# One load of second weights per step, another order of SyncE's transfers, and own buffers for the rows of half slots, in a kernel of attention and routed experts

## The reference

```python
# x: 4 x 1024 tokens of 256 features, float32
x = x + attn(layernorm(x))      # 16 heads of 16, rotary positions, causal, softmax, projection
x = x + experts(layernorm(x))

def experts(x):                 # 4096 tokens, 8 experts, 256 -> 1024 -> 256
    aff = x @ centroids.T
    assign = argmax(aff, axis=1)                 # one expert per token
    alpha = sigmoid(aff[assign])
    h = layernorm(x, ln_g[assign], ln_b[assign])
    y = x + relu(h @ w1[assign].T + b1[assign]) @ w2[assign].T + b2[assign]
    return alpha * y + (1 - alpha) * x
```

## Time and profile before

| | us |
|---|---|
| median of 3 runs (lowest, highest) | 881.75 (878.6, 885.98) |
| the profiled execution, its own time | 886.25 |
| its span, from the first to the last instruction | 884.5 |
| TensorE busy in the span | 812.1 (92%) |
| VectorE busy | 599.5 (68%) |
| ScalarE busy | 508.4 (57%) |
| GpSimd busy | 340.6 (39%) |
| mean granted clock of TensorE | 0.967 |

### The profile page before, as it was taken

How to read it: one execution, slowest core, us unless ns; L and a number is a source line. 1 busy time by engine, 2 the same in 40 slices (tenths; PEclk the granted TensorE clock), 3 DMA queues, 4 the chain that set the end, 5 groups by cost and what they waited for, 6 DMA issues and landing times. The chain is left out here.

```text
span 884.5 us, 24359 instructions
## 1 busy us (share of the span) xinstructions
PE 812.1 (92%) x8788; PEld 497.3 (56%) x8789; DVE 599.5 (68%) x1161; ACT 508.4 (57%) x1175; POOL 340.6 (39%) x476
## 2 busy tenths in 40 slices
PE   7999859889979999999999988777999999999984
PEld 4555423333334444443344335456999999999853
DVE  5888999779969999999999605754733333333342
ACT  4767427668858888888888892023333333333331
POOL 9999653233333433334343332524111111133211
PEclk9999979999989999999999999988899999999998
DMA  7578532543453343433335115865555555555550
GB/s 281 179 231 255 170 119 69 175 169 53 111 106 91 95 100 97 90 87 86 86 81 159 51 42 180 277 189 196 173 186 182 180 180 183 187 187 189 179 173 4
DMA packets 63355, 128.90 MB, mean 146 GB/s; under 512 B 16982, under 2 KB 44247, under 8 KB 56983
## 3 DMA queue, kind: packets, MB, share of 16 engines
q1 hardware_dynamic: 59094, 112.53, 42.9%
q0 software_dynamic: 4160, 15.03, 4.6%
HBM read 99.89 MB, written 22.98 MB: 139 GB/s over the span
## 5 line engine op out<-in xcount | busy, mean ns | idle before, releaser
L917 ACT ACTIVATE arena<-ps_pair 128x512 f32<-128x512 f32 (+2 forms) x640 | 317.9, 556 | 76.6 <-PE ps_pair L1240 73.7
L997 DVE TENSOR_REDUCE B_block_max<-ps_item 128x8 f32<-128x1024 f32 x288 | 335.4, 1217 | 37.4 <-PE ps_item L1144 37.1
L1240 PE MATMUL ps_pair<-q_stack,k_stack 99*32 99x512 bf16 (+7 forms) x3072 | 198.5, 334 | 9.4 <-DMA q_stack<-B_nm 6.7
L831 POOL TENSOR_SCALAR_AFFINE_SELECT arena<-arena 128x256 f32<-128x256 f32 x256 | 102.4, 409 | 160.2 <-ACT arena L917 158.5
L1257 PE MATMUL ps_pair<-arena,B_v_quad 128*32 128x512 f32 (+3 forms) x1536 | 157.0, 493 | 0.9 <-ACT B_oacc L936 0.7
L1240 PEld LDWEIGHTS ps_pair<-q_stack,k_stack 99*32 99x32 bf16 (+1 forms) x3072 | 69.1, 96 | 130.0 <-ACT arena L917 62.1
L2037 PEld LDWEIGHTS C_bank<-arena 128*128 128x128 f32 x1024 | 122.5, 196 | 5.2 <-ACT arena L1558 3.7
L2037 PE MATMUL C_bank<-arena 128*128 128x128 f32 x1024 | 123.0, 280 | 2.0 <-ACT arena L1558 2.0
L1144 PE MATMUL ps_item<-k_stack,q_stack 64*128 64x128 bf16 (+2 forms) x1280 | 108.2, 267 | 15.9 <-DVE B_block_max L997 8.9
L2061 PE MATMUL C_ps_p<-arena 128*128 x512 | 117.4, 381 | 3.2 <-issue 3.1
L1588 ACT ACTIVATE arena<-C_bank,ffn_columns 128x128 f32<-128x128 f32 x128 | 36.6, 368 | 116.8 <-PE C_bank L2037 108.0
(11 more groups left out here) (204 smaller groups left out, 777.0 us busy)
## 6 DMA issues: line engine op xcount, KB each, us to landing
arena<-in_w_exp SPq DMA_DIRECT2D x41, 1024.0 KB
qk_parts<-arena SPq DMA_DIRECT2D x32, 384.0 KB, 3.4
q_stack<-qk_parts SPq DMA_DIRECT2D x96, 128.0 KB, 3.3
k_stack<-qk_parts SPq DMA_DIRECT2D x64, 128.0 KB, 3.4
arena<-in_w_exp POOLq DMA_DIRECT2D x6, 1024.0 KB, 7.1
rows<-payload SPq DMA_DIRECT2D x32, 130.5 KB
arena<-in_x SPq DMA_DIRECT2D x8, 512.0 KB, 4.7
arena<-in_x_feat SPq DMA_DIRECT2D x8, 512.0 KB, 5.7
```

The costliest lines, as they stand in the source:

```text
L831: pool.affine_select(out=block_p, in_=block_p, compare_op=ALU.is_ge, fill=0.0, base=0, pattern=[[0, 2], [1, P]], channel_multiplier=-1).th ...
L917: act.activation(pr[s % PR][:, h:h + 2 * n - 1:2, 0:W], ps_s[(EXPS * Q.const + exps_to[s] + u) % R][:, 0:n * W].rearrange("p (h n) -> p h ...
L997: dve.tensor_reduce(bmx[:, g:QH:GH, first:first + 3 * gap + 1:gap], src[:, :, :].rearrange("p c (b n) -> p c b n", n=P), AX.X, ALU.max).th ...
L1240: mm = pe.matmul(bank[at:at + 32, :], ks[rows, r, half, bass.ds(g * SEQ + kb * P + at, 32)], qs[rows, r, half, bass.ds(g * SEQ + c * QW + ...
```

## The change

In attention, the six early loads of second weights go out one to a step (steps 1, 2, 3, 4, 5 and 14) instead of in pairs (1, 1, 2, 2, 14, 14), and in sub-step 4 instead of sub-step 2. SyncE's step issues the rows of maxima ahead of `place_out` instead of behind it, and `spread_inverse` ahead of the pad rows; these are written three in each of steps 5, 7 and 9 instead of nine in step 4. In the expert phase, each half slot has its own buffer for its rows and a semaphore of its own, and they are loaded one half slot a step in steps 24 to 30, behind the loads of the step, with no wait for a result.

```diff
+        half_rows = ctx.enter_context(nc.sbuf_tensor("half_rows", [P, HALVES, P + PAYW - DIM], F32))
+        def load_half_rows(sp, k):
+            at = sp.value_load(slot_tab[0:1, 1, bass.ds(FULL + k, 1)], min_val=0, max_val=DUMMY_ROW + HT)
+            sp.dma_start(half_rows[:, k, 0:P],
+                         pay_d[bass.ds(at, HT), 0:DIM].rearrange("t (a n) -> a t n", a=DC)).then_inc(s_rh[k], 16)
+            sp.dma_start(half_rows[:, k, P:P + PAYW - DIM],
+                         pay_d[bass.ds(at, HT), DIM:PAYW].unsqueeze(0).to_broadcast([DC, HT, PAYW - DIM])).then_inc(s_rh[k], 16)
...
-        early_at = (1, 1, 2, 2, 14, 14)
+        early_at = (1, 2, 3, 4, 5, 14)
+        W2_AT = 4
...
                     if n.const >= 3:
                         store_inverse(sp, n.const - 3)
-                    if n.const >= 2:
-                        place_out(sp, n.const - 2, out_ring(n.const - 2))
                     if n.within(NQ):

                         wait(sp, s_n3, n, 1, 1)
                         for half in range(2):
                             sp.dma_start(qs[SROWS[half]:SROWS[half] + MROWS, n.ring(R), half, :],
                                          nm[half * MAXR // 2:(half + 1) * MAXR // 2, :]).then_inc(s_row, 16)
+                    if n.const >= 2:
+                        place_out(sp, n.const - 2, out_ring(n.const - 2))
                     if n.const == 2:
                         load_bias_rows(sp)
-                    if n.const == 4:
-                        sp.wait_ge(s_pad0, 2)
-                        for e in range(NE + 1):
-                            sp.dma_start(pay_d[e * REGION:e * REGION + P, :], padrow).then_inc(s_pad, 16)
                     if n.const >= 3:
                         spread_inverse(sp, n.const - 3)
+                    if n.const in (5, 7, 9):
+                        if n.const == 5:
+                            sp.wait_ge(s_pad0, 2)
+                        for e in range(3 * (n.const - 5) // 2, 3 * (n.const - 5) // 2 + 3):
+                            sp.dma_start(pay_d[e * REGION:e * REGION + P, :], padrow).then_inc(s_pad, 16)
...
-                        if k == NM_AT + 1:
+                        if k == W2_AT:
...
-                    if S.within(NSLOT):
+                    if S.within(NSLOT) and not is_half(S):
...
+                    if n.reg is None and COPY_AT <= n.const < COPY_AT + HALVES:
+                        load_half_rows(sp, n.const - COPY_AT)
```

More of the change, by code:

```diff
@@ L347, in program @@
         rows = ctx.enter_context(nc.sbuf_tensor("rows", [P, RD, PAYW], F32))
+        half_rows = ctx.enter_context(nc.sbuf_tensor("half_rows", [P, HALVES, P + PAYW - DIM], F32))
+        s_rh = [sem(f"half_rows_loaded{k}") for k in range(HALVES)]
         def load_rows(sp, S):
-            at = sp.value_load(slot_tab[0:1, 1, bass.ds(S.value(), 1)], min_val=0,
-                               max_val=DUMMY_ROW + (HT if is_half(S) else 0))
-            if is_half(S):
-                sp.dma_start(rows[:, S.ring(RD), 0:HT * 2],
-                             pay_d[bass.ds(at, HT), 0:DIM].rearrange("t (a n) -> a t n", a=DC)).then_inc(s_rl[S.ring(RD)], 16)
-                sp.dma_start(rows[:, S.ring(RD), DIM:PAYW],
-                             pay_d[bass.ds(at, HT), DIM:PAYW].unsqueeze(0).to_broadcast([DC, HT, PAYW - DIM])).then_inc(s_rl[S.ring(RD)], 16)
-            else:
-                sp.dma_start(rows[:, S.ring(RD), :], pay_d[bass.ds(at, P), :]).then_inc(s_rl[S.ring(RD)], 16)
@@ new lines, in row_data, with row_scalar, wait_rows @@
+        def row_data(S):
+            return half_rows[:, S.const - FULL, 0:P] if is_half(S) else rows[:, S.ring(RD), 0:DIM]
+        def row_scalar(S, c):
+            if is_half(S):
+                return half_rows[:, S.const - FULL, c - P:c - P + 1]
+            return rows[:, S.ring(RD), c:c + 1]
+        def wait_rows(eng, S):
+            if is_half(S):
+                eng.wait_ge(s_rh[S.const - FULL], 32)
+            else:
+                wait_dma(eng, s_rl, S)
+        phase_route_experts(nc, x, pay_d, load_w1, load_rows, load_half_rows, row_data, row_scalar, wait_rows, w2s, w1b, s_w1, cols, b2, cst, ident, eps, slot_tab, col, b2r,
@@ L1273, in _, with phase_route_experts @@
                 steps(pe, emit)
-def phase_route_experts(nc, x, pay_d, load_w1, load_rows, rows, s_rl, w2s, w1b, s_w1, cols, b2, cst, ident, eps, slot_tab, col, b2r,
+def phase_route_experts(nc, x, pay_d, load_w1, load_rows, load_half_rows, row_data, row_scalar, wait_rows, w2s, w1b, s_w1, cols, b2, cst, ident, eps, slot_tab, col, b2r,
                         wp, bp3, ones3, xl, o_feat, room, spare_room, s_b3, out, gate,
@@ L1528, in normalize @@
                     if S.within(NSLOT):
-                        wait_rows(act, s_rl, S)
+                        wait_rows(act, S)
                         wait(act, s_tx, S, 1, -1)
                         wait(act, s_tl, S, 1, -1)
-                        row = rows[:, S.ring(RD), :]
                         n = P if is_half(S) else DIM
-                        act.activation(zz[:, S.ring(2), 0:n], row[:, 0:n], ACT.Identity, bias=row[:, COL_B:COL_B + 1],
-                                       scale=row[:, COL_S:COL_S + 1]).then_inc(s_zz, 1)
+                        act.activation(zz[:, S.ring(2), 0:n], row_data(S), ACT.Identity, bias=row_scalar(S, COL_B),
+                                       scale=row_scalar(S, COL_S)).then_inc(s_zz, 1)
                 for w in range(NP):
@@ L1604, in emit @@
                     if S.within(NSLOT):
-                        wait_rows(act, s_rl, S)
+                        wait_rows(act, S)
                         wait(act, s_res, S, 1, -1)
-                        act.activation(al[:, S.ring(2), 0:1], rows[:, S.ring(RD), COL_GATE:COL_GATE + 1], ACT.Exp,
+                        act.activation(al[:, S.ring(2), 0:1], row_scalar(S, COL_GATE), ACT.Exp,
                                        scale=-1.0).then_inc(s_ex, 1)
@@ L1833, in tail @@
                     if S.within(NSLOT):
-                        row = rows[:, S.ring(RD), :]
                         wait(dve, s_zz, S, 1, 1)
                         n = P if is_half(S) else DIM
-                        dve.scalar_tensor_tensor(out=row[:, 0:n], in0=zz[:, S.ring(2), 0:n], scalar=row[:, COL_K:COL_K + 1], in1=row[:, 0:n],
+                        dve.scalar_tensor_tensor(out=row_data(S), in0=zz[:, S.ring(2), 0:n], scalar=row_scalar(S, COL_K), in1=row_data(S),
                                                  op0=ALU.mult, op1=ALU.add).then_inc(s_tl, 1)
@@ L1870, in keep_ids @@
                 def keep_ids(S):
-                    at = rows[:, S.ring(RD), COL_ID:COL_ID + 1].bitcast(I32)
+                    at = row_scalar(S, COL_ID).bitcast(I32)
                     if is_half(S):
@@ L1924, in emit @@
                         dve.scalar_tensor_tensor(out=res[:, S.ring(2), 0:k], in0=y[:, S.ring(2), 0:k], scalar=al[:, S.ring(2), 2:3],
-                                                 in1=rows[:, S.ring(RD), 0:k],
+                                                 in1=row_data(S),
                                                  op0=ALU.mult, op1=ALU.add).then_inc(s_res, 1)
```

9 lines of the change are left out of this document (2 added, 7 removed).

## The result

The changed kernel takes 912.3 us at the median of four runs (903.01 to 913.61), the kernel before 881.46 beside it (878.6 to 885.98): a ratio of 1.0298, with a 95% interval of 1.0253 to 1.0343. It is 3% slower, where 877 was predicted and 889 was the top of the range. The profiled execution took 913.61 us, span 911.9.

What follows compares the result with a forecast made beforehand. TensorE was taken as the bound, busy in attention steps of 23.90 us except for 18.7 us of stalls, and idle in the half slots. Gains of 0.1 (attention) + 4.5 (half slots) = 4.6 us from 881.75 gave 877, range 863 to 889.

Steps and rivals of the forecast that it cites:

- Order on SyncE: Attention: outputs placed behind the rows of maxima delay the stack load; 3.6 us over eight ordinary steps, 2.2 in step 2.
- the price of 0.45 us a step: Ordinary attention steps: cost of the new SyncE order, taken as 0.45 us between bounds of 0 and 1.1.
- the landing left at 2.3 us: End of the stack load: its last transfer lands 2.3 us after issue, with 0.5 us added for step 5.
- the clock counted outside of the chain: Attention stalls: three of four long ones drop TensorE's clock, 3 x 1.75 = 5.3 us, bounds 0 and 7.
- SyncE's queue becomes the bound and the kernel gets slower: Rival, attention: outputs behind the rows push the stack load to the end of every step; 894 (882 to 896), chance 0.12.
- Second weights: Attention steps 1, 2 and 14: one load a step removes all three waits for the rows of maxima, 10.3 us.
- Pad rows: Attention: step 4's loss of 8.07 us goes; three pad rows cost 2.35 us in each of steps 5, 7 and 9.
- Half slots: End of the expert phase: own buffers remove TensorE's idle time between 844 and 868; 4.5 us gained.
- The clock holds: Rival, attention: the four stalls stay under what drops TensorE's clock; 870, chance 0.26.
- All as written: Rival, whole change: SyncE's queue keeps up and no stack is late; 23.2 us less, 858.5, chance 0.11.
- Rows late for another reason: Rival, attention steps 1, 2 and 14: weights do not cause the waits, so 10.3 us come back; 887, chance 0.05.
- It decides for slower when steps 2 to 13 lose over 1.9 us each: Attention: the slower rival's threshold, average loss a step with clock included, 18.7 + 4.5 us over twelve steps.

Runs made afterwards that it cites:

- Kernels 8 to 10: The first: changed kernel with the spreading of the inverse sums moved into SyncE's idle time ahead of the rows of maxima, ratio 0.9897; the others: kernel 9, kernel 10.
- kernel 9: Changed kernel with the spreading moved ahead of the rows of maxima and a 32-byte transfer in its former place; ratio to the kernel before 0.9957.
- kernel 11: Changed kernel plus six filler matmuls on TensorE ahead of item 0's wait for the stack, steps 2 to 14; ratio to the kernel before 1.0236.
- kernel 12: Changed kernel plus twelve filler matmuls on TensorE ahead of item 0's wait for the stack, steps 2 to 14; ratio to the kernel before 1.0224.
- kernel 2: Kernel before with only the second weights changed, one load a step in sub-step 4; ratio to the kernel before 0.9949.
- kernel 5: Changed kernel with the old order on SyncE, outputs placed ahead of the rows of maxima again; ratio to the kernel before 0.9849.
- kernel 3: Kernel before with only the pad rows changed, three in each of steps 5, 7 and 9; ratio to the kernel before 0.9927.
- kernel 7: Changed kernel with outputs ahead of the rows of maxima again and the one weight load a step in sub-step 2; 850.06 us, ratio 0.9730.
- kernel 10: As kernel 7, but SyncE waits for TensorE's release before the spreading, which then goes directly ahead of the stack load; ratio to the kernel before 0.9998.

## Why the prediction was wrong, point by point

**The step that failed is "Order on SyncE"**, and in it three values: the price of 0.45 us a step, the landing left at 2.3 us, and the clock counted outside of the chain. The rival "SyncE's queue becomes the bound and the kernel gets slower" is what happened, in its place and by the first part of its mechanism (the outputs push the stack load to the end of every step); its 894 was too low, and its chance of 0.12 too small. Its second part, stacks behind three pad rows that land like step 4's, did not come: the last transfers of steps 5, 7 and 9 landed in 2.9, 3.0 and 3.4 us.

*Price.* The text had worked out a chain of 25.0 us from the rows of step 6 and then took 0.45 in place of 1.1, because at plain issues it would fit. The measured chain is never within the beat. In step 6, which has neither weights nor pad rows, it is 27.4 us: 25.0 as worked out, 2.1 more for the maxima and 0.7 more for the last landing, less 0.5, because the outputs took 5.0 us and not 5.6. The upper bound was the forecast to take: the load's issues took 9.6 us in this step and not the plain 8.3.

*Landing.* 2.3 us was the value of a queue that had stood idle for 2.6 us before the load. In the new order outputs, spreading and stack follow without a gap; the last transfers (line 401) land in 4.0 us at the median where line 391 had 2.4. Kernels 8 to 10 show that the 256 KB directly ahead are the cause, in either order. This is the largest single share: kernel 9 has nearly the issues of the changed kernel and 35 us less in attention. The text costed the outputs and the spreading by SyncE's issue alone, and asked what bytes do to those behind them only for the pad rows and for the load of step 5. The row that would have told was there: the earlier trace rows have landings of 5.6 us behind the nine pad rows, and that was put down to the pads alone.

*Clock.* It was priced as a surcharge on a stall, 1.75 us, "with bounds 0 and 7". But TensorE's work between item 0 and the maxima lies in the chain that leads to the next stack load. Most stalls slow it, by up to 2.3 us (7.0 from item 0 to the maxima, where behind the wait of 0.94 it was 4.75), which makes the next stack late: each stall pays for the next. Kernels 11 and 12 bear that out; the 12.6 us of kernel 12 hang on it, in one execution of each.

These do not add up separately. Once the chain is over the beat, each microsecond in it costs one in each of eleven steps and may set off the clock too; below the beat it costs nothing. The 0.6 us of issue and 256 KB of one transfer swing 39 us.

*Second weights.* That the three waits go was right; that nothing comes in their place was not. The load lies beside the stack load, which the text saw for step 5 alone and priced at 0.5: kernel 2 kept 5.3 of the 10.3, and in kernel 5 steps 3 to 5 lose 2.9, 2.9 and 4.7. "SyncE has by then issued the rows" looked only at the queue it left, not at the one it met.

*Pad rows.* The 8.07 go, as written (31.97 becomes 23.90 in kernel 3). Their cost of 2.35 a step was for a chain without slack: kernels 3 and 5 show next to nothing in the old order. In the new one they are 1.4 us of issue in steps 5, 7 and 9.

*Half slots.* Right: 5.2 us alone, 5.1 in their stretch (forecast 4.5), TensorE busy throughout, and the scatter does not bound.

*The rivals.* "The clock holds": refuted, ten stalls drop it. "All as written": kernel 7 shows that it was to be had, at 2.7%, with the old order and sub-step 2. "Rows late for another reason": refuted, no `q_stack<-B_nm` wait is left. "It decides for slower when steps 2 to 13 lose over 1.9 us each": the maxima of steps 2 and 14 are 342.1 us apart, 55.3 over twelve beats of 23.90, so they lost 4.6 each.

**Left open.** Why 256 KB in front slow all of the 1.5 MB behind them: a transfer held to a quarter of the engines is the likely reason, and a spreading laid out in another shape would test it. What the pauses in mid-step of kernel 5 are. And why the rest of the program, outside of attention, differs by 15.5 us between the profiled executions of kernels that are alike in it (486.9 in kernel 7, 502.4 in kernel 10); the attention stretch is therefore the surer measure of the two in the table.

## What to carry to other kernels

When transfers change places on a queue, cost the bytes as well as the issues: ask what is in flight when each one starts, and take a landing time only from a row where the same things stand in front of it. A gap on a queue that looks idle may be what keeps the landing behind it short. And before pricing a stall, see whether the work that follows it leads to the next one: if it does, a chain just over the beat costs its excess in every step and the low clock on top, so the upper bound is the forecast. Large loads go where no one waits for a small one, which is a window to be read from landings, not from issues.

## What the runs showed of the hardware

- One transfer of 256 KB directly ahead of fourteen transfers of 64 and 128 KB, on the same queue, raised the median landing of the 128 KB ones from 2.9 to 4.4 us (in the step shown from 2.8 to 5.3, and the engines' time for a megabyte from 56 to 85 engine-microseconds). With 2.6 us of gap it was 3.8. By itself this transfer kept the 16 engines 0.19 to 0.25 busy for some four microseconds.
- A load of 1 MB on GpSimd's queue landed in 5.2 to 6.0 us with little beside it (kernels 5 and 7), and in 12.9, 11.8 and 12.4 us beside a stack load on SyncE's; a 64 KB transfer issued on SyncE's queue just after such a load took 7.3 us instead of some 2.3.
- In the changed kernel TensorE's granted clock, averaged over the five microseconds behind a wait, was 0.50 to 0.54 of full speed (1.2 GHz is 0.50) after waits of 3.48 us and more, 0.66 after those of 1.90, 2.27, 2.51 and 3.31, and 1.00 after those of 0.94 and 1.10. The length of the wait alone does not decide it: with filler ahead of it the clock stayed at 1.00 after 2.25 us and was 0.50 after 2.48 (kernel 11). A matmul filler of 2.4 us ahead of the wait made the kernel faster although it added work.
